# Registers loaded for four experts at once and nested size conditions in a mixture-of-experts kernel

## The reference, cut to what matters

```python
scores = softmax(x @ gate_w.T); topk_w, topk_idx = top_k(scores, 6)
C = 384                                  # slots of an expert; rows over it are dropped
buf[e, pos] = x[token]                   # tokens sorted by expert
g = einsum('ecd,efd->ecf', buf, w_gate); u = einsum('ecd,efd->ecf', buf, w_up)
eo = einsum('ecf,edf->ecd', silu(g) * u, w_down)      # F = 176, D = 256
y[token] += eo[e, pos] * weight
```

## Time and profile before

| | us |
|---|---|
| median of three runs | 636.83 |
| the profiled execution | 634.79 |
| its span, first to last instruction | 633.1 |
| start of the gate product of the first expert, of the last expert | 235.61, 598.48 |
| PE busy, of the span | 529.2 |
| POOL busy, DVE busy, ACT busy | 301.6, 306.1, 190.2 |

### The profile page before, as it was taken

How to read it: one execution, slowest core, us unless ns; L and a number is a source line. 1 busy time by engine, 2 the same in 40 slices (tenths; PEclk the granted TensorE clock), 3 DMA queues, 4 the chain that set the end, 5 groups by cost and what they waited for, 6 DMA issues and landing times.

```text
span 633.1 us, 13037 instructions
## 1 busy us (share of the span) xinstructions
PE 529.2 (84%) x2669; PEld 396.2 (63%) x2670; DVE 306.1 (48%) x814; ACT 190.2 (30%) x398; POOL 301.6 (48%) x251
## 2 busy tenths in 40 slices
PE   0899998989999978999887988797877988899930
PEld 0535454353455557898766867686766877788920
DVE  8635558574782224444442543343534444535515
ACT  0112212211301113344432443342433343434410
POOL 6001027477576721477643553354445353746640
PEclk9899899999999999999987999797999899989975
DMA  6829949487424325899976987786877787988759
GB/s 202 247 86 350 298 130 310 156 281 252 142 106 141 116 89 129 184 200 193 206 191 163 194 200 168 179 197 142 188 180 180 183 180 186 220 226 186 135 110 333
DMA packets 87780, 119.62 MB, mean 189 GB/s; under 512 B 12480, under 2 KB 73648, under 8 KB 87664
## 3 DMA queue, kind: packets, MB, share of 16 engines
q1 hardware_dynamic: 65632, 85.46, 45.7%
q0 software_dynamic: 22032, 32.85, 25.8%
HBM read 78.88 MB, written 39.39 MB: 187 GB/s over the span
## 4 chain that ended last, share of the span: by engine, by line
PE 46%; SPq 23%; issue 15%; DVE 10%; DMA 5%; ACT 1%; POOLq 0%; POOL 0%; DVEq 0%
PE bank L1075 11%; SPq L403 6%; SPq L313 6%; PE bank L1015 5%; PE bank L936 5%; PE bank L886 4%; PE bank L1105 4%; PE bank L1106 4%; PE bank L1027 3%; SPq L394 3%; SPq L371 3%; SPq L370 3%; PE bank L957 3%; DMA wt<-in_wdt 2%; DVE M L749 2%
## 5 line engine op out<-in xcount | busy, mean ns | idle before, releaser
L511 POOL DMA_INDIRECT acc<-sil,sids x64 | 97.4, 1522 | 104.3 <-ACT sil L599 92.2
L511 POOL DMA_INDIRECT acc<-OH,sids x63 | 95.8, 1521 | 89.4 <-ACT OH L599 73.0
L494 POOL DMA_INDIRECT slot_rows<-ctok,sli x96 | 94.8, 987 | 81.3 <-DVE sli L689 51.3
L1075 PE MATMUL bank<-xgT,wb 128*128 128x192 f32 (+5 forms) x456 | 92.7, 358 | 28.7 <-issue 16.3
L1075 PEld LDWEIGHTS bank<-xgT,wb 128*128 128x128 f32 (+1 forms) x456 | 77.3, 196 | 38.2 <-issue 32.5
L850 DVE TENSOR_TENSOR hh<-sg,bank 48x384 f32<-48x384 f32 x64 | 35.6, 556 | 112.4 <-ACT sg L588 112.3
L1106 PE MATMUL bank<-wt,hh 128*128 128x256 f32 x276 | 82.7, 381 | 0.0
L586 ACT ACTIVATE sg<-bank 128x384 f32<-128x384 f32 x64 | 31.4, 491 | 93.5 <-PE bank L1075 93.5
L1106 PEld LDWEIGHTS bank<-wt,hh 128*128 128x128 f32 x276 | 53.0, 192 | 7.4
L1075 PE MATMUL bank<-xT_g,hT 128*128 128x192 f32 (+5 forms) x228 | 46.4, 358 | 8.4 <-DMA wt<-in_wdt 5.6
L1075 PE MATMUL bank<-x_g,h0T 128*128 128x256 f32 (+5 forms) x204 | 42.4, 360 | 8.3 <-DMA wt<-in_wdt 6.0
(11 more groups left out here) (180 smaller groups left out, 683.4 us busy)
## 6 DMA issues: line engine op xcount, KB each, us to landing
cw<-in_cW SPq DMA_DIRECT2D x64, 256.0 KB, 3.9
wb<-in_wblk SPq DMA_DIRECT2D x32, 496.0 KB
cw<-slot_rows SPq DMA_DIRECT2D x94, 136.0 KB
h0T<-in_wblk SPq DMA_DIRECT2D x16, 496.0 KB
hT<-in_wblk SPq DMA_DIRECT2D x16, 496.0 KB
acc<-zrow POOLq DMA_DIRECT2D x2, 2432.0 KB
slot_rows<-blank SPq DMA_DIRECT2D x64, 68.0 KB, 3.2
cw<-acc SPq DMA_DIRECT2D x8, 512.0 KB, 6.0
```

Source lines behind the costliest of these rows:

```text
L494: pool.indirect_dma_start(slots_d, bass.IndirectOffsetOnAxis(sli[:, g % 2, k, t:t + 1], 0), ctok[:, g % 2, t, :], None, bounds_check=SLOTS ...
L511: pool.indirect_dma_start(acc[u % 2], bass.IndirectOffsetOnAxis(sids[0:rows, u % SR, j:j + 1], 0), yo[u % UE][0:rows, j, :], None, compute ...
L1075: ins = mm(bank[o][0:m, lo:hi], w(b, c), xgT[u % UE][:, c, lo:hi], start=c == 0, stop=c == DC - 1)
```

## The change

One register-load instruction brings in the values of four neighbouring experts, without the check of their range; SIZE and UNUSED are read so, LANDED as before. GATHERED is gone: SP adds 16 for each piece that isn't there to the semaphore on which PE waits, with a semaphore instruction, so that PE waits for a constant (48 more for each expert). The conditions for the pieces are nested. The DVE instructions that made GATHERED are gone, and SP, PE and POOL wait for the part of `facts` that they read. All transfers stay in SP's queue, in the same order.

```diff
-        def by_pieces(eng, size, work):
-            with eng.If(size > 0):
+        def by_pieces(eng, size, work, done):
+            with eng.If(size > 1):
                 work(0, P)
+                with eng.If(size > 2):
+                    work(1, P)
+                    with eng.If(size > 3):
+                        with eng.If(size > 4):
+                            work(2, P)
+                        with eng.Else():
+                            work(2, H)
+                    with eng.Else():
+                        eng.sem_inc(done or s_tick, 16)
+                with eng.Else():
+                    work(1, H)
+                    eng.sem_inc(done or s_tick, 16)
             with eng.Else():
-                work(0, H)
-            for j in range(1, TJ):
-                with eng.If(size > 2 * j):
-                    work(j, P)
+                with eng.If(size > 0):
+                    work(0, P)
                 with eng.Else():
-                    with eng.If(size > 2 * j - 1):
-                        work(j, H)
-                    with eng.Else():
-                        eng.sem_inc(s_tick, 1)
+                    work(0, H)
+                eng.sem_inc(done or s_tick, 32)
...
             def get(what, e, u):
-                if (what, u) not in known:
-                    known[what, u] = eng.value_load(facts[0:1, what, bass.ds(e, 1)], min_val=0, max_val=SLOTS - H if what == UNUSED else 16 * (TJ * E + TJ))
-                return known[what, u]
+                lead = u % READ
+                if (what, u - lead) not in known:
+                    known[what, u - lead] = nc.values_load_multi_w_load_instructions(
+                        facts[0:1, what, bass.ds(e - lead, READ)], engines=[eng.engine],
+                        skip_runtime_bounds_check_because="a count of conditions, or a row number clamped to the table by the minimum with CAP")[1]
+                return known[what, u - lead][lead]
...
-            sp.wait_ge(s_flags, 1)
+            sp.wait_ge(s_flags, 2)
...
-                by_pieces(sp, size, load)
+                by_pieces(sp, size, load, s_xg[u % UE])
...
-            pool.wait_ge(s_flags, 1)
+            pool.wait_ge(s_flags, 3)
...
-                size, landed = get(SIZE, e, u), get(LANDED, e, u)
+                size, landed = get(SIZE, e, u), pool.value_load(facts[0:1, LANDED, bass.ds(e, 1)], min_val=16, max_val=16 * (TJ * E + TJ))
...
-            flink(v.tensor_scalar(last_wait[:, :], seen[:, E - 2:E], 16.0, 16.0, ALU.mult, ALU.add))
-            for u in range(UE):
-                last = v.tensor_tensor_scan(seen[:, u:E:UE], onesf[:, 0:E:UE], tiles_f[:, u:E:UE], 0.0, ALU.mult, ALU.add)
-            flink(last)
-            v.tensor_scalar(facts[:, GATHERED, :], seen[:, :], 16.0, None, ALU.mult).then_inc(s_flags, 1)
+            v.tensor_scalar(last_wait[:, :], seen[:, E - 2:E], 16.0, 16.0, ALU.mult, ALU.add).then_inc(s_flags, 1)
...
-                gathered = get(GATHERED, e, u)
                 size = get(SIZE, e, u)
-                pe.wait_ge(s_xg[u % UE], gathered)
+                pe.wait_ge(s_xg[u % UE], (16 * TJ // UE) * (e - u % UE + UE))
...
-            pe.wait_ge(s_flags, 1)
+            pe.wait_ge(s_flags, 2)
```

More of the change, by code:

```diff
@@ L56 @@
 SIZES = [n * H for n in range(1, CAP // H + 1)]
-SIZE, LANDED, GATHERED, UNUSED = range(4)
+SIZE, UNUSED, LANDED = range(3)
+READ = 4
 assert TJ * P == CAP and G * GT == N
@@ L170, in program @@
         wt = [wt4[:, i, :] for i in range(UE)]
-        facts = sb("facts", [P, 4, E], I32)
+        facts = sb("facts", [P, 3, E], I32)
         unused = sb("unused", [P, E])
@@ L518, in scatters @@
                 pool.sem_inc(s_tick, 1)
-                by_pieces(pool, size, scatter)
+                by_pieces(pool, size, scatter, None)
             def step(e, u):
@@ L787, in _ @@
                 group(g)
-            steps = [0]
+            steps = [1]
             def flink(ins):
@@ L795, in flink @@
                 dve.wait_ge(s_fl, steps[0])
-            steps[0] = 1
             dve.wait_ge(s_fl, 1)
-            with nc.allow_low_precision(reason="counts up to 4 are exact"):
-                v.reduce_sum(facts[:, SIZE, :], more[:, :, :].rearrange("p i e -> p e i"), AX.X)
-            v.tensor_tensor(facts[:, UNUSED, :], unused[:, :], e_off[:, :], ALU.add)
+            with nc.allow_low_precision(reason="counts up to 5 are exact"):
+                v.reduce_sum(facts[:, SIZE, :], more[:, :, :].rearrange("p i e -> p e i"), AX.X).then_inc(s_flags, 1)
+            v.tensor_tensor(facts[:, UNUSED, :], unused[:, :], e_off[:, :], ALU.add).then_inc(s_flags, 1)
             flink(v.tensor_tensor(tiles_f[:, :], more[:, SIZES.index(P), :], more[:, SIZES.index(2 * P), :], ALU.add))
```

## The result

The changed kernel takes 589.88 us (median of 4 runs, 588.2 to 592.43) beside 637.52 us of the kernel before on the same chip; the ratio is 0.925, with an interval from 0.920 to 0.931. That is 47.6 us less, where 35 were forecast; the time lies in the range of 588 to 622 us, 1.9 us above its lower end, outside the narrower 591 to 612 us that the forecast gave as its own, and close to the 587 us of the rival "PE alone". The profiled execution took 588.67 us, its span 587.0.

A forecast was written before the change was run, and what follows sets the result against it. SP's queue was taken to bound the experts' stage. Possible gains were SP 54, PE 50, DMA engines 35 to 49 us; the smallest decided: 634.8 - 35 + 2.0 = 601.8 us, own range 591 to 612, wider range 588 to 622.

The forecast's parts named there:

- PE alone: Rival: the DMA engines do 210 GB/s, so only PE limits the stage of the experts; 587 us, chance 0.10.
- The bound: Stage of the experts: SP's queue getting through its instructions, not arithmetic or bandwidth, sets the pace, 6.02 us a step.
- The price of a read and of the conditions: SP's queue: one single-value read costs 0.66 us, two a step 1.32; nesting the conditions saves 0.33 us a step.
- The load of four: SP's queue: loading four registers takes 0.27 to 1.09 us, middle 0.68, so loads save 0.80 us a step.
- The lead: Seven loads ahead of step 0 get faster by 1.1 us each, 8 us in all, without shortening the time.
- PE: Stage of the experts: products, transposes, branch stops and first steps need 312.5 us against 362.9, a gain of 50 at most.
- The DMA engines: Stage of the experts: 67.0 MB at 201 GB/s take 333 us, gaining 35; at 210 GB/s 319, gaining 49.
- Contention at 622 us: Rival: closer issues lengthen the landing of weights, the stage moves 190 GB/s and gains 15 us; chance 0.14.
- The costly load: Rival: on SP a load of four costs as much as four whole reads, 2.64 us; 629 us, chance 0.06.
- the costly jumps over the longer arms: Rival: jumps over longer nested arms force instruction fetches on SP, 2.40 us a step; 61 us more, 698 us, chance 0.05.

The follow-up runs named there:

- the written-out kernel: The changed kernel with all 64 steps written out, no loop: 664.06 us beside 731.1 for the kernel before, ratio 0.907.

## Why the prediction was right, point by point

*The bound.* Right. SP's queue held the stage: the loads of four make 45 us with SP's among them and none on PE and POOL alone, and reads given back to SP take 38 of the 50 us of the stage away.

*The price of a read and of the conditions.* 0.66 us a read stood well: with two more of them SP's first 48 steps take 5.93 us each, 1.2 above the 4.7 that SP needs in the changed kernel where it waits for nothing. They cost 38 us of the stage and not 48 x 1.3 = 62, since the changed kernel's 48 steps take 5.14 us each on that chip with their waits for PE. The 16 us for the branches were 20 us in all and 16 in the stage.

*The load of four.* A term that was mis-sized: I took the middle, 0.68 us, between one load and four. It takes 0.31 us, 0.04 more than a load of one, so it lay at the low end of the bounds. With it SP's step comes to 6.02 - 1.32 + 9/16 x 0.55 - 0.33 = 4.68 us instead of 4.89, and 4.7 is what the ten steps from 336.29 us show. The Trainium skill gives 200 ns for each register (Runtime: NRT & Kernel Launch, Instruction fetch mechanics), and the same page's section "Terms" says that its loads bring registers from HBM. For `facts`, a tile in SBUF, the rows do not agree with that figure: three registers more cost 39 ns together. This changed nothing in the sum, as SP was not the smallest term.

*The lead.* The seven loads ahead of step 0 were to get 8 us faster in all, which would be only lead. SP's first step starts at 243.86 instead of 248.34 us, 4.5 us earlier, and the first gate-up stays where it was.

*PE.* Right. Its sum was 312.5 us from the first to the last gate-up, and 316.0 were measured. The stops at the branches, said to be hidden before and to count after, are there: 5.42 and 3.54 us idle, and the first gate-ups behind take 5.15 us, at a clock of 0.50, and 4.29 us. The two steps at each branch (318.83 to 336.32 and 399.74 to 416.57 us) take 34.3 us from gate-up to gate-up where their products sum to 21.2, so 13.1 us over it, where 13.5 were forecast, and the written-out kernel gives 14.7 back. The reads on PE are covered.

*The DMA engines.* The range holds the time, but this step failed. The prediction took 201 GB/s, read where PE was never idle and the share was 0.92, for what the engines can do, made of it a gain of 35 us, and let this term decide as the smallest. But in that stretch PE was the limit, so the rate was what PE and SP asked for, not what the engines could give. The changed kernel moves 242 to 248 GB/s in two such stretches, and with less work for PE 233 over the whole stage. A share of 0.92 did not mean that 8% were left: the whole stage of the written-out kernel has a share of 0.92 too, at 217 GB/s. The kernel before could have warned of it. Its stretches without a gap in PE lie between 167 and 210 GB/s, and the fastest of all its stretches of 16 us from 237 to 589 us is one in which PE was idle for a quarter of the time:

```profile
541.00:557.00 16.00, 12.25 (x64) 10.74 (x63) 6.59 (x19) 5.96 (x13) 10.61 (x7) 0.97 0.96 220
```

That the stage after moves 205 GB/s, about the 200 that the prediction named, says nothing for its reason: it is the 67 MB over the time that PE needs. With 240 GB/s the term is 67.0 / 0.240 = 279 us, a gain of 89, and the smallest term is PE's: 587 us, where 589.88 were measured. So the term put the forecast 15 us above PE's sum, and that sum was 3.5 us too low, which leaves 12: 601.8 against 589.9. The rival "PE alone", given a chance of 0.10, should have been the forecast. That the range of 588 to 622 us holds the time is in part luck: the mechanism that decided was priced at 587 us, just outside it.

*The rivals.* Contention at 622 us did not come: SP's transfers do hold its queue longer at times, as in this row of the changed kernel's timeline, where 0.34 us is usual, but PE waits for weights by name only once; weights are issued four experts ahead.

```profile
427.54 1.32 SPq L383 DMA_DIRECT2D wt<-in_wdt  x1
```

The costly load and the costly jumps over the longer arms did not come either; a taken branch inside a step still costs 0.18 us by the chain of the changed kernel (0.05 for L299 at 354.21 us and 0.13 of issue behind it).

## What to carry to other kernels

When the chain of waits runs through a queue that issues transfers, price its register loads, checks, branches and address arithmetic like work, for here they added up to more than the transfers (some 55% of the chain in the earlier trace rows against 38.5%); take them out by loading several values at once, nesting conditions, or writing the loop out. Before naming the next limit from a rate, ask who set that rate: a bandwidth read where another engine was the bound is a demand and not a capacity. A stop that costs nothing beside a slower queue, as PE's backward branch seems to have here, comes back once that queue is fast: 13 us of the changed kernel.

## What the runs showed of the hardware that was not expected

- A load of four registers on SP takes 0.312 us, of one 0.273; on PE it is 0.338 against 0.306, on POOL 0.327 against 0.294.
- PE's backward branch holds its sequencer for 3.7 to 6.4 us in the kernels with the full body, but in the kernel with half of the gate-up products only for 0.21 us (the third in each is the way out):

```profile
L339 PEldq COMPARE_BRANCH  x3: 76/208/217, 398.7 to 546.0; - x3
```

  Its body has fewer instructions, and PE idles more there; which of the two it is wasn't tried.
- On the two other chips the first stage takes some 94 us longer in every kernel, and in it DVE stands for long with nothing in the profile that it waits for, as here between two of its own instructions in the kernel with the loads of four alone. There 22 us of DVE's waits in the first stage are such "issue", and 72 us are put down to "remote", a release for which the profile has no instruction; the kernel before on the first chip has none of the latter and 0.4 us of the former. What holds it is open.

```profile
105.33 0.42 DVE L737 COPY Ls<-bank 128x256 f32<-128x256 f32 x1 [10.80 <-issue]
```
